# Decoded feed-forward weights stored whole in pass one, their block sums formed in pass two

## The chip, the core and the metric

The kernel runs on one core of one Trainium2 chip. The metric is the device time of one execution in microseconds, the median over several runs.

## What is computed

A transformer block with adaptive layer norm over 4 x 512 tokens of 1024 features: modulation vectors from a small matrix product, layer norm, a block-masked 1024 x 1024 product with a gated residual, layer norm, and a gated feed-forward network whose weights are stored as 4-bit codes with a scale for each 64 entries.

```python
mod = (_silu(L0_c) @ L0_wmod).reshape(L0_c.shape[0], 6, 1, -1)
sa, ca, ga, sb, cb, gb = (mod[:, 0], mod[:, 1], mod[:, 2], mod[:, 3], mod[:, 4], mod[:, 5])
...
h = _layernorm(x, axis=-1) * (1 + ca) + sa
x = x + ga * _L0_attn_ref(h, L0_attn_weight, L0_attn_mask)
h = _layernorm(x, axis=-1) * (1 + cb) + sb
x = x + gb * _L0_ffn_ref(h, L0_ffn_w1_q, ..., L0_ffn_w3_scale)
...
# in _L0_ffn_ref: w1, w2 of 2752 x 1024 and w3 of 1024 x 2752, decoded from codes and scales
h = jax.nn.silu(jnp.einsum('bsd,hd->bsh', x, w1)) * jnp.einsum('bsd,hd->bsh', x, w2)
return jnp.einsum('bsh,dh->bsd', h, w3)
```

## The kernel before

The five engines run programs written out by hand, each in its own order; they meet at semaphores (`wait_ge`, `then_inc`). Every DMA is issued by SyncE, whose queue is as strict in its order as the engines' programs: an issue that waits holds up all issues behind it. Each float32 product is made of three matmuls on a high part (rounded, made mostly by ScalarE) and a low part (the rest, made by VectorE).

The hidden dimension of 2752 is cut into 21 chunks of 128 (`FULL`) and a tail of 64.

**Pass one** (`up_group`) multiplies w1 and w2 with batches 0 and 1. For chunk c ScalarE decodes the codes of chunk c+1 by eight `lines` and VectorE scales and splits them (`finish`). The decoded tiles `RAW` (128 x 8 x 128 for w1 and for w2) are needed again in pass two, so what pass two wants of them is written to `t_d` in HBM.

**Pass two** (L1787) does the other two batches with seven block products for each chunk (`UP`: m5, m2, m1, m4, m6, m3, m7, a Strassen scheme over the two halves of the feature dimension, w1 against w2 and the two batches) in place of eight. Five of the seven weight operands are sums or differences of two blocks of 128 x 512, two (m4, m3) are a plain block. Before the change VectorE forms the sums in pass one (`sums`, buffers `TS`), and pass two loads one finished operand for each product (`load_stream`). They lie in buffers `TT[c % 2][i]`, i from 0 to 6 in the order of `UP`, each with a high part at its start and a low part behind it, over which the raw operand lands. ScalarE makes the high part (`stream_high`), VectorE the low part (`stream_low`, called a split below), one chunk ahead of TensorE. Of the seven results, ScalarE copies m5 and m2 out of PSUM (`copy_up`), VectorE adds the others to four tiles (`use_m1` two operations, `use_m4` two, `use_m6` one, `use_m3` two, `use_m7` one); then ScalarE applies silu (`silu_up`) and VectorE multiplies (`make_h_up`), in the next chunk. The input side of the seven products, `XC`, is formed once where pass two begins (`x_add`, `x_high`, `x_low`).

Beside this, pass two decodes w3: after the high parts of its chunk ScalarE runs eight steps on 128 x 1024 (`w3_lines`, L804), one block of w3 for each chunk and two in chunks 5 and 13 (`w3_jobs`); VectorE scales it (`w3_combine`, L1458); SyncE stores it, loads the next scales, and has the loads of streams 5 and 6 behind that store (`finish_w3` at i == 4).

ScalarE's program in a chunk of pass two is:

```python
silu_up(c - 1, 1)
silu_up(c - 1, 0)
stream_high(c + 1, 0)
copy_up(c, "m5")
for i in range(1, 4):
    stream_high(c + 1, i)
copy_up(c, "m2")
for i in range(4, NU):
    stream_high(c + 1, i)
...
for j in w3_jobs(c):
    w3_lines(j)
```

**The down projection** (`down_tile`) comes last. Its first loads, `t_raw` from w3 and `s_raw` from h, are issued in the last chunk of pass two behind the last `finish_w3`.

Of the kernel before, what the change touches and what calls it, by code (L numbers as in the profile page):

```python
# [23 lines left out]
P = 128  # L24
# [4 lines left out]
C = D // P  # L29
# [47 lines left out]
def adaln_kernel(nc, cT, x, w12q, w12s, w3q, w3s, wT, maskT, wmod, out):  # L77
# [41 lines left out]
    TS = [at(f"combined_{i}", [HALF_C, P], F32, 120 + 2 * i) for i in range(4)]  # L119
# [74 lines left out]
    t_d = nc.dram_tensor("t_d", (CH * NU * P, HALF_C * P), F32, kind="Internal").ap()  # L194
# [8 lines left out]
    ts_added, tt_hi, tt_lo = sem("ts_added"), sem("tt_hi"), sem("tt_lo")  # L203
    first_stored = sem("first_stored")
    ts_stored = [sem(f"ts_stored_{i}") for i in range(4)]
# [102 lines left out]
    FROM_W1, FROM_BOTH = ["m5"], ["m2", "m1", "m6", "m7"]  # L308
    FIRST_AT = 10
    SUMS = []  # L310
    for step in range(FULL):
        tile = step + 1
        SUMS += [(tile, "m2")] if tile == FULL else [(tile, name) for name in FROM_W1]
        if step == FIRST_AT:
            SUMS += [(0, name) for name in FROM_W1 + FROM_BOTH]
        if tile < FULL:
            SUMS += [(tile, name) for name in FROM_BOTH]

    def sums_through(n):
        return max(q for q, (tile, _) in enumerate(SUMS) if tile == n) + 1  # L320

# [79 lines left out]
    with block:  # L401

        @block.sync
        def _(sp):
# [10 lines left out]
            def load_codes(n, w):  # L415
                r = ring(n, w)
                if n >= 3:
                    sp.wait_ge(w12_lo, 2 * (n - 2) + 2)
                    sp.wait_ge(ts_added, sums_through(n - 2))
# [99 lines left out]
            def t_rows(n, name):  # L519
                row = (n * NU + UP_AT[name]) * P  # L520
                return t_d[row:row + P, :]

            def store_part(n, w, half):
                name = {0: "m3", 1: "m4"}[half]
# [6 lines left out]
                sp.dma_start(t_rows(n, name), src[:, half * HALF_C:(half + 1) * HALF_C, :].rearrange("p c k -> p (c k)")).then_inc(done, 16)  # L531
# [79 lines left out]
            for w in range(2):  # L611
                store_part(0, w, w)
            for c in range(FULL):
# [6 lines left out]
                store_part(n, 0, 0)  # L620
                if n == FULL:
                    store_part(n, 0, 1)
                store_sum(n, "m2" if n == FULL else "m5")
                if 1 <= c <= HALF_TILES - 2:
                    load_normed(c + 1)
                if c == FIRST_AT:
                    for name in FROM_W1 + FROM_BOTH:
                        store_sum(0, name)
                if n < FULL:
                    store_part(n, 1, 1)  # L630
                    if n + 1 < FULL:
                        load_s12(n + 1, 1)
                    store_sum(n, "m2")
                store_h(c, 0)
                if n < FULL:
                    store_sum(n, "m1")
                    store_sum(n, "m6")
                store_h(c, 1)
                if n < FULL:
                    store_sum(n, "m7")  # L640

                if c == FULL - 1:
                    sp.wait_ge(first_stored, 32)
                    for i in range(2):
                        load_stream(0, i)
                    for r in range(4):
                        sp.wait_ge(pure_stored[r], 16 * (12 if r == 2 else 10))
                        sp.wait_ge(ts_stored[r], 16 * len(range(r, len(SUMS), 4)))
                    for i in range(2, NU):
# [132 lines left out]
        def _(act):  # L782
# [163 lines left out]
            def stream_high(c, i):  # L946
                act.wait_ge(tt_loaded[c % 2][i], 16 * (c // 2 + 1))
                act.activation(TT[c % 2][i][0], TT[c % 2][i][2], ACT.Copy).then_inc(tt_hi, 1)  # L948

            def copy_up(c, name):  # L950
                p, i = c % 2, UP_AT[name]
                act.wait_ge(up_m_done, NU * c + i + 1)
                if c == 0:
                    for q in (2, 3):
                        act.wait_ge(ts_stored[q], 16 * len(range(q, len(SUMS), 4)))
                elif name == "m5" and c >= 2:
# [104 lines left out]
        def _(dve):  # L1061
# [15 lines left out]

            def sums(n, names):
                for name in names:
                    q = SUMS.index((n, name))  # L1080
                    if q >= 4:
                        dve.wait_ge(ts_stored[q % 4], 16 * (q // 4))
                    parts, sign = (((0, 0), (0, 1)), 1) if n == FULL else UP[UP_AT[name]][1:3]
                    if n == 0:
                        dve.wait_ge(raw_restored, 2)
                    src = [(RAW0[w] if n == 0 else RAW[ring(n, w)])[:, HALF_C * half:HALF_C * (half + 1), :] for w, half in parts]
                    dve.tensor_tensor(TS[q % 4][:], src[0], src[1], ALU.add if sign > 0 else ALU.subtract).then_inc(ts_added, 1)

# [258 lines left out]
            def early_x(c):  # L1347
# [4 lines left out]
                elif c == 14:  # L1352
                    dve.wait_ge(ts_added, sums_through(0))
# [4 lines left out]
            for c in range(FULL):  # L1358
                n = c + 1
                finish(n, 0)  # L1360
                sums(n, ["m2"] if n == FULL else FROM_W1)
                if 1 <= c <= HALF_TILES:
                    modulate_half(HALF_TILES + c - 1)
                if c == FIRST_AT:
                    sums(0, FROM_W1 + FROM_BOTH)
# [496 lines left out]
```

## Time and profile before

| | |
|---|---|
| median of 3 runs | 1634.79 us (1633.08 to 1635.11) |
| the profiled execution's own time | 1632.93 us |
| its span, mean granted clock of TensorE | 1630.9 us, 0.984 |
| TensorE matmul | 1553.4 us busy, 95% |
| VectorE | 1036.3 us busy, 64% |
| ScalarE | 988.0 us busy, 61% |
| DMA | 345.97 MB, mean 212 GB/s |

The span is the time from the first to the last instruction of the profiled execution. A busy share is a mean over stages: TensorE's is full in the three long stages and broken at the start and at the hand-overs from stage to stage. Matmuls of 128 x 512 overlap, so their pace is read from start to start and not from the length of one.

### The profile page before, as it was taken

The numbers are of one execution on the slowest core, as the hardware profiler recorded it, in microseconds if no ns is written. First come the engines' busy times: TensorE is split into PE (matmuls) and PEld (weight loads), VectorE is DVE, ScalarE is ACT, GpSimd is POOL, SyncE is SP. The second block draws the span as 40 slices with busy tenths as digits, with TensorE's granted clock in tenths as the row PEclk, the third lists the DMA queues.
The fourth block names the chain that finished last, engine by engine and source line by source line (L and its number), as shares of the span: only waits on it lengthen the run. The fifth ranks groups of instructions, "written<-read, shape, count | busy, mean of one in ns | idle before, by whom it ended". The sixth has DMA issues, their size and how long they took to land.

```text
span 1630.9 us, 19164 instructions
## 1 busy us (share of the span) xinstructions
PE 1553.4 (95%) x7216; PEld 1274.2 (78%) x7216; DVE 1036.3 (64%) x1494; ACT 988.0 (61%) x1280; POOL 10.6 (1%) x11
## 2 busy tenths in 40 slices
PE   2889999999999999999899999999969999999998
PEld 1667778888888888888688888888858888888886
DVE  3677687665545565444756566566676757867777
ACT  2445666898888888882777877877633333323320
POOL 1100000000000000000000000000000000000000
PEclk9899999999999999999999999999989999999999
DMA  9873421465446554442666766676587958958865
GB/s 370 336 257 136 169 90 63 174 213 178 166 156 207 174 174 153 151 152 97 212 202 194 232 210 215 207 234 230 174 309 301 315 176 298 360 180 298 308 220 196
DMA packets 170091, 345.97 MB, mean 212 GB/s; under 512 B 14728, under 2 KB 65288, under 8 KB 170000
## 3 DMA queue, kind: packets, MB, share of 16 engines
q1 hardware_dynamic: 170000, 344.76, 61.5%
q8 instruction: 57, 0.93, 0.2%
q14 instruction: 34, 0.28, 0.1%
HBM read 249.77 MB, written 94.93 MB: 211 GB/s over the span
## 4 chain that ended last, share of the span: by engine, by line
PE 63%; ACT 19%; DVE 10%; issue 4%; DMA 3%; SPq 1%; DVEq 0%; ACTq 0%
ACT w_raw L804 10%; PE ps L1746 9%; PE ps L1747 9%; PE ps L1748 9%; PE ps L1816 9%; PE ps L1817 9%; PE ps L1818 9%; ACT stream_hi L948 4%; DVE stream_lo L1380 2%; DVE up_c L1396 2%; DMA wmod<-wmod 2%; PE ps L1681 2%; PE ps L1683 2%; PE ps L1682 2%; PE ps L1645 2%
## 5 line engine op out<-in xcount | busy, mean ns | idle before, releaser
L794 ACT ACTIVATE w_raw<-w_raw 128x1024 f32<-128x1024 f32 x287 | 304.8, 1062 | 9.1
L1746 PE MATMUL ps<-ffn_in_hi,w_hi 128*128 128x512 f32 x688 | 268.6, 390 | 0.0
L1748 PE MATMUL ps<-ffn_in_hi,w_lo 128*128 128x512 f32 x688 | 267.8, 389 | 0.0
L1747 PE MATMUL ps<-ffn_in_lo,w_hi 128*128 128x512 f32 x688 | 267.7, 389 | 0.0
L1816 PE MATMUL ps<-t_hi,s_hi 128*128 128x512 f32 x616 | 240.5, 390 | 13.9 <-DVE s_lo L1504 13.9
L1760 PE MATMUL ps<-x_m_hi,stream_hi 128*128 128x512 f32 x604 | 236.5, 392 | 8.2 <-DVE x_m_lo L1345 4.8
L1817 PE MATMUL ps<-t_lo,s_hi 128*128 128x512 f32 x616 | 240.4, 390 | 0.0
L1818 PE MATMUL ps<-t_hi,s_lo 128*128 128x512 f32 x616 | 240.3, 390 | 0.0
L1762 PE MATMUL ps<-x_m_hi,stream_lo 128*128 128x512 f32 x604 | 236.3, 391 | 0.0
L1761 PE MATMUL ps<-x_m_lo,stream_hi 128*128 128x512 f32 x604 | 236.3, 391 | 0.0
L1010 ACT ACTIVATE s_hi<-s_raw 128x1408 fp32r<-128x1408 f32 x56 | 77.5, 1383 | 232.2 <-DVE s_raw L1499 189.5
L804 ACT ACTIVATE w_raw<-w_raw 128x1024 f32<-128x1024 f32 (+1 forms) x154 | 163.5, 1061 | 4.9
L1066 DVE SCALAR_TENSOR_TENSOR w_raw<-w_raw,w_scale 128x1024 f32<-128x1024 f32 x41 | 50.3, 1226 | 175.0 <-ACT w_raw L794 175.0
L1748 PEld LDWEIGHTS ps<-ffn_in_hi,w_lo 128*128 128x128 f32 x688 | 129.1, 188 | 27.0
L1746 PEld LDWEIGHTS ps<-ffn_in_hi,w_hi 128*128 128x128 f32 x688 | 129.2, 188 | 26.5
L1747 PEld LDWEIGHTS ps<-ffn_in_lo,w_hi 128*128 128x128 f32 x688 | 129.2, 188 | 26.5
L1816 PEld LDWEIGHTS ps<-t_hi,s_hi 128*128 128x128 f32 x616 | 116.1, 189 | 38.6 <-DVE s_lo L1504 14.3
L1760 PEld LDWEIGHTS ps<-x_m_hi,stream_hi 128*128 128x128 f32 x604 | 114.1, 189 | 33.6 <-issue 10.0
L1817 PEld LDWEIGHTS ps<-t_lo,s_hi 128*128 128x128 f32 x616 | 116.1, 188 | 24.1
L1818 PEld LDWEIGHTS ps<-t_hi,s_lo 128*128 128x128 f32 x616 | 116.0, 188 | 24.1
L1762 PEld LDWEIGHTS ps<-x_m_hi,stream_lo 128*128 128x128 f32 x604 | 114.1, 189 | 23.9
L1761 PEld LDWEIGHTS ps<-x_m_lo,stream_hi 128*128 128x128 f32 x604 | 114.0, 189 | 23.9
(127 smaller groups left out, 2097.3 us busy)
## 6 DMA issues: line engine op xcount, KB each, us to landing
s_raw<-h_d SPq DMA_DIRECT2D x96, 704.0 KB, 5.5
stream_raw<-t_d SPq DMA_DIRECT2D x150, 256.0 KB, 4.9
t_d<-combined SPq DMA_DIRECT2D x106, 256.0 KB, 2.6
wmod<-wmod SPq DMA_DIRECT2D x12, 2048.0 KB, 16.1
t_raw<-w_d SPq DMA_DIRECT2D x88, 256.0 KB, 6.4
w_codes<-w12q SPq DMA_DIRECT2D x41, 512.0 KB, 5.2
h_d<-h_tile SPq DMA_DIRECT2D x44, 256.0 KB, 2.4
w_d<-w_raw SPq DMA_DIRECT2D x22, 512.0 KB, 3.0
```

What stands on the lines that cost most here:

```text
L794: act.activation(RAWF[r], RAWF[r] if j else RQ[r][:], ACT.Prelu, bias=bias, scale=sign, alpha=slope).then_inc(line_ready, 1)
L804: act.activation(E3[p][0:rows, :], (E3 if j else E3Q)[p][0:rows, :], ACT.Prelu, bias=bias, scale=sign, alpha=slope).then_inc(w3_line, 1)
L1010: act.activation(SH[p][:], SR[p][:, 1], ACT.Copy).then_inc(s_hi, 1)
L1746: pe.matmul(acc, RH[r][:, k, :], HH[:, b, k, :], start=(k == 0), stop=False)
L1747: pe.matmul(acc, RH[r][:, k, :], HL[:, b, k, :], start=False, stop=False)
L1748: last = pe.matmul(acc, RL[r][:, k, :], HH[:, b, k, :], start=False, stop=(k == C - 1))
L1760: pe.matmul(acc, th[:, k, :], xh[:, k, :], start=(first and k == 0), stop=False)
L1761: pe.matmul(acc, th[:, k, :], xl[:, k, :], start=False, stop=False)
L1762: last = pe.matmul(acc, tl[:, k, :], xh[:, k, :], start=False, stop=(stop and k == HALF_C - 1))
L1816: pe.matmul(acc, SH[p][:, k, :], TH[i % 2][k][:], start=(k == 0), stop=False)
L1817: pe.matmul(acc, SH[p][:, k, :], TL[i % 2][k][:], start=False, stop=False)
L1818: last = pe.matmul(acc, SL[p][:, k, :], TH[i % 2][k][:], start=False, stop=(k == HC - 1))
```

## The change

Pass one stores the decoded tiles as they are, two of 512 KB for each chunk (`store_raw`), and forms no sums; `TS` and its semaphores are gone. In pass two each of the five combined operands is loaded as two raw blocks, one in the place of the low part as before, the other (`second`) in the place of the high part, and VectorE adds or subtracts them in place (`stream_add`) before ScalarE makes the high part over the second block. Each call of `stream_low` first does the add of the next operand in the order of the stream and then its own split. `stream_high` waits for the add (`tt_added`) where it waited for the load. Besides, `w3_combine` moves from behind `use_m6` to behind `use_m7`, and the first two loads of pass two no longer go ahead of the waits for pass one's stores. The programs of TensorE and ScalarE keep their order.

```diff
     def halves(name, kb, n):
...
-                at(name + "_raw", [HALF_C, n], F32, lo_kb)[:])
+                at(name + "_raw", [HALF_C, n], F32, lo_kb)[:], at(name + "_second", [HALF_C, n], F32, kb)[:] if n == P else None)
...
+    STREAM = [(c, i) for c in range(FULL) for i in range(NU)] + [(FULL, i) for i in (1, 3, 5)]
+
+    def weight_parts(c, i):
+        if c == FULL:
+            return {1: ((0, 0), (0, 1)), 3: ((0, 1),), 5: ((0, 0),)}[i]
+        return UP[i][1]
...
-            def store_part(n, w, half):
+            def store_raw(n, w):
...
-            def store_sum(n, name):
-                q = SUMS.index((n, name))
-                sp.wait_ge(ts_added, q + 1)
-                sp.dma_start(t_rows(n, name), TS[q % 4][:].rearrange("p c k -> p (c k)")).then_inc(ts_stored[q % 4], 16)
+                sp.dma_start(t_rows(n, w), src[:].rearrange("p c k -> p (c k)")).then_inc(done, 16)
...
             def load_stream(c, i):
                 if c >= 2:
                     sp.wait_ge(up_m_done, NU * (c - 2) + i + 1)
-                sp.dma_start(TT[c % 2][i][2].rearrange("p c k -> p (c k)"), t_rows(c, UP[i][0])).then_inc(tt_loaded[c % 2][i], 16)
+                for n, (w, half) in enumerate(weight_parts(c, i)):
+                    dst = TT[c % 2][i][2 + n]
+                    sp.dma_start(dst.rearrange("p c k -> p (c k)"), t_rows(c, w)[:, half * HALF:(half + 1) * HALF]).then_inc(tt_loaded[c % 2][i], 16)
...
             def stream_high(c, i):
-                act.wait_ge(tt_loaded[c % 2][i], 16 * (c // 2 + 1))
+                if len(weight_parts(c, i)) == 2:
+                    act.wait_ge(tt_added, stream_sums(c, i))
+                else:
+                    act.wait_ge(tt_loaded[c % 2][i], 16 * (c // 2 + 1))
                 act.activation(TT[c % 2][i][0], TT[c % 2][i][2], ACT.Copy).then_inc(tt_hi, 1)
...
             for c in range(FULL):
                 n = c + 1
                 finish(n, 0)
-                sums(n, ["m2"] if n == FULL else FROM_W1)
...
                 if n < FULL:
                     finish(n, 1)
-                    sums(n, FROM_BOTH[:1])
                 make_h(c, 0)
-                if n < FULL:
-                    sums(n, FROM_BOTH[1:3])
                 make_h(c, 1)
-                if n < FULL:
-                    sums(n, FROM_BOTH[3:])
-
-            def stream_low(c, i):
+
+            def stream_add(c, i):
+                parts = weight_parts(c, i)
+                if len(parts) == 2:
+                    dve.wait_ge(tt_loaded[c % 2][i], 32 * (c // 2 + 1))
+                    op = ALU.add if c == FULL or UP[i][2] > 0 else ALU.subtract
+                    t = TT[c % 2][i]
+                    dve.tensor_tensor(t[2], t[2], t[3], op).then_inc(tt_added, 1)
+
+            def stream_split(c, i):
                 dve.wait_ge(tt_hi, stream_at(c, i) + 1)
                 t = TT[c % 2][i]
                 dve.tensor_tensor(t[1], t[2], t[0].bitcast(F32), ALU.subtract).then_inc(tt_lo, 1)
 
+            def stream_low(c, i):
+                at_ = stream_at(c, i)
+                if at_ + 1 < len(STREAM):
+                    stream_add(*STREAM[at_ + 1])
+                stream_split(c, i)
+
+            stream_add(0, 0)
             for i in range(4):
                 stream_low(0, i)
...
                 use_m4(c)
                 use_m6(c)
-                for j in w3_jobs(c)[:1] if c else ():
-                    w3_combine(j)
                 for i in range(4, 6) if c else range(6):
                     stream_low(c + 1, i)
                 use_m3(c)
                 stream_low(c + 1, 6)
                 use_m7(c)
-                if c == 0:
-                    w3_combine(0)
-                for j in w3_jobs(c)[1:]:
+                for j in w3_jobs(c):
                     w3_combine(j)
```

What this makes of the order on the engines is seen at three places. In the names, `stream_04` is operand 4 of an even chunk, `stream_14` of an odd one, `raw`, `second`, `hi` and `lo` are its parts; line numbers are those of each kernel.

VectorE in a chunk of pass two, from `use_m6` on (`up_c...<-up_c...,ps`), before the change:

```order
L1396 TENSOR_TENSOR up_c22_1_169<-up_c22_1_169,ps 128x512
L1458 SCALAR_TENSOR_TENSOR w3_raw_0_174<-w3_raw_0_174,w3_scale_178 128x1024
L1380 TENSOR_TENSOR stream_04_lo_117<-stream_04_raw_118,stream_04_hi_116 128x512
L1380 TENSOR_TENSOR stream_05_lo_120<-stream_05_raw_121,stream_05_hi_119 128x512
L1396 TENSOR_TENSOR up_c22_1_169<-up_c22_1_169,ps 128x512
L1396 TENSOR_TENSOR up_c12_1_171<-up_c12_1_171,ps 128x512
L1380 TENSOR_TENSOR stream_06_lo_123<-stream_06_raw_124,stream_06_hi_122 128x512
L1396 TENSOR_TENSOR up_c11_1_167<-up_c11_1_167,ps 128x512
L1449 TENSOR_TENSOR up_c22_1_169<-up_c12_1_171,up_c22_1_169 128x512
L1449 TENSOR_TENSOR up_c21_1_173<-up_c11_1_167,up_c21_1_173 128x512
L1380 TENSOR_TENSOR stream_10_lo_126<-stream_10_raw_127,stream_10_hi_125 128x512
L1380 TENSOR_TENSOR stream_11_lo_129<-stream_11_raw_130,stream_11_hi_128 128x512
```

and with the change, where L1336 is the add and L1341 the split:

```order
L1364 TENSOR_TENSOR up_c22_1_179<-up_c22_1_179,ps 128x512
L1341 TENSOR_TENSOR stream_04_lo_117<-stream_04_raw_118,stream_04_hi_116 128x512
L1336 TENSOR_TENSOR stream_06_raw_126<-stream_06_raw_126,stream_06_second_127 128x512
L1341 TENSOR_TENSOR stream_05_lo_121<-stream_05_raw_122,stream_05_hi_120 128x512
L1364 TENSOR_TENSOR up_c22_1_179<-up_c22_1_179,ps 128x512
L1364 TENSOR_TENSOR up_c12_1_181<-up_c12_1_181,ps 128x512
L1336 TENSOR_TENSOR stream_10_raw_130<-stream_10_raw_130,stream_10_second_131 128x512
L1341 TENSOR_TENSOR stream_06_lo_125<-stream_06_raw_126,stream_06_hi_124 128x512
L1364 TENSOR_TENSOR up_c11_1_177<-up_c11_1_177,ps 128x512
L1426 SCALAR_TENSOR_TENSOR w3_raw_1_185<-w3_raw_1_185,w3_scale_188 128x1024
L1417 TENSOR_TENSOR up_c22_1_179<-up_c12_1_181,up_c22_1_179 128x512
L1417 TENSOR_TENSOR up_c21_1_183<-up_c11_1_177,up_c21_1_183 128x512
```

Add 6 now stands between the splits of operands 4 and 5, behind `use_m6`; the add of operand 0 for the chunk after stands ahead of split 6; and the combine has moved behind `use_m7`, directly ahead of the two multiplications of `make_h_up`.

VectorE where pass two begins, from the first split to the first `x_add`, before the change:

```order
L1380 TENSOR_TENSOR stream_00_lo_105<-stream_00_raw_106,stream_00_hi_104 128x512
L1380 TENSOR_TENSOR stream_01_lo_108<-stream_01_raw_109,stream_01_hi_107 128x512
L1380 TENSOR_TENSOR stream_02_lo_111<-stream_02_raw_112,stream_02_hi_110 128x512
L1380 TENSOR_TENSOR stream_03_lo_114<-stream_03_raw_115,stream_03_hi_113 128x512
L1335 TENSOR_TENSOR x_m1_raw_154<-ffn_in_raw_00_51,ffn_in_raw_11_54 128x2048
```

and with the change:

```order
L1336 TENSOR_TENSOR stream_00_raw_102<-stream_00_raw_102,stream_00_second_103 128x512
L1336 TENSOR_TENSOR stream_01_raw_106<-stream_01_raw_106,stream_01_second_107 128x512
L1341 TENSOR_TENSOR stream_00_lo_101<-stream_00_raw_102,stream_00_hi_100 128x512
L1336 TENSOR_TENSOR stream_02_raw_110<-stream_02_raw_110,stream_02_second_111 128x512
L1341 TENSOR_TENSOR stream_01_lo_105<-stream_01_raw_106,stream_01_hi_104 128x512
L1341 TENSOR_TENSOR stream_02_lo_109<-stream_02_raw_110,stream_02_hi_108 128x512
L1336 TENSOR_TENSOR stream_04_raw_118<-stream_04_raw_118,stream_04_second_119 128x512
L1341 TENSOR_TENSOR stream_03_lo_113<-stream_03_raw_114,stream_03_hi_112 128x512
L1297 TENSOR_TENSOR x_m1_raw_164<-ffn_in_raw_00_51,ffn_in_raw_11_54 128x2048
```

Four adds have come between, and the last of them is that of operand 4, which needs the eighth and ninth load.

SyncE around the store of a decoded w3 block in pass two, before the change:

```order
L554 DMA stream_04_raw_118<-t_d 128x512
L562 DMA w3_codes_1_177<-w3q 128x1024
L572 DMA w3_d<-w3_raw_0_174 128x1024
L567 DMA w3_scale_178<-w3s 64x1024 x2
L554 DMA stream_05_raw_121<-t_d 128x512
L554 DMA stream_06_raw_124<-t_d 128x512
L554 DMA stream_10_raw_127<-t_d 128x512
```

and with the change:

```order
L543 DMA stream_04_raw_118<-t_d 128x512
L543 DMA stream_04_second_119<-t_d 128x512
L551 DMA w3_codes_0_186<-w3q 128x1024
L561 DMA w3_d<-w3_raw_1_185 128x1024
L556 DMA w3_scale_188<-w3s 64x1024 x2
L543 DMA stream_05_raw_122<-t_d 128x512
L543 DMA stream_06_raw_126<-t_d 128x512
L543 DMA stream_06_second_127<-t_d 128x512
L543 DMA stream_10_raw_130<-t_d 128x512
L543 DMA stream_10_second_131<-t_d 128x512
```

The two loads behind the w3 store are three now, and operand 0 of the next chunk takes two as well.

## Rows read from the trace of the kernel before

**Rows 1.** Busy time by stretch: from:to, length, busy per engine, clock, DMA, GB/s

```profile
475.00:660.00 185.00, 185.00 (x822) 153.31 (x821) 98.66 (x121) 152.65 (x157) 0.00 (x0) 1.00 0.51 169
802.44:1157.33 354.89, 354.89 (x1567) 293.85 (x1566) 217.73 (x334) 278.98 (x370) 0.00 (x0) 1.00 0.67 215
1066.00:1085.00 19.00, 19.00 (x85) 15.75 (x84) 11.96 (x19) 14.52 (x20) 0.00 (x0) 1.00 0.85 284
```

**Rows 2.** What TensorE waited for: total us, times, longest

```profile
PE ps L1816 <- DVE s_lo L1504: 13.9, 1, 13.9
PE ps L1760 <- DVE x_m_lo L1345: 4.8, 3, 1.9
```

**Rows 3.** ScalarE in order of time, one chunk: start, length, [idle before <-releaser]

```profile
842.77 0.64 ACT L972 ACTIVATE up_c<-up_c 128x512 f32<-128x512 f32 x1 [3.69 <-DVE up_c L1396]
...
847.07 0.59 ACT L962 ACTIVATE up_c<-ps 128x512 f32<-128x512 f32 x1
847.54 1.67 ACT L948 ACTIVATE stream_hi<-stream_raw 128x512 fp32r<-128x512 f32 x3
849.11 1.06 ACT L804 ACTIVATE w_raw<-w_codes 128x1024 f32<-128x1024 int32 x1
...
867.85 1.06 ACT L804 ACTIVATE w_raw<-w_codes 128x1024 f32<-128x1024 int32 x1
```

**Rows 4.** VectorE in order of time, the same chunk

```profile
847.74 1.29 DVE L1396 TENSOR_TENSOR up_c<-ps,up_c 128x512 f32<-128x512 f32 x2 [0.89 <-ACT up_c L962]
848.95 1.28 DVE L1380 TENSOR_TENSOR stream_lo<-stream_raw,stream_hi 128x512 fp32r<-128x512 f32 x2
850.15 1.88 DVE L1396 TENSOR_TENSOR up_c<-up_c,ps 128x512 f32<-128x512 f32 x3
857.85 1.23 DVE L1458 SCALAR_TENSOR_TENSOR w_raw<-w_raw,w_scale 128x1024 f32<-128x1024 f32 x1 [5.83 <-ACT w_raw L804]
858.99 1.29 DVE L1380 TENSOR_TENSOR stream_lo<-stream_raw,stream_hi 128x512 fp32r<-128x512 f32 x2
```

**Rows 5.** TensorE in order of time: start of chunk 1, end of the tail

```profile
796.63 0.63 PE L1762 MATMUL ps<-x_m_hi,stream_lo 128*128 128x512 f32 x1
797.06 0.46 PE L1760 MATMUL ps<-x_m_hi,stream_hi 128*128 128x512 f32 x1
...
1188.61 0.39 PE L1762 MATMUL ps<-x_m_hi,stream_lo 128*128 128x512 f32 x1
```

**Rows 6.** Groups by line, shapes apart: the in-place add of the down projection

```profile
L1511 DVE TENSOR_TENSOR t_raw<-t_raw 128x512 f32<-128x512 f32 x55 | 37.4, 688 | 25.4 <-DMA t_raw<-w_d 25.4
```

**Rows 7.** SyncE's queue in order of time, after a combine

```profile
860.76 1.55 SPq L554 DMA_DIRECT2D stream_raw<-t_d  x3
```

**Rows 8.** DMA issues of the page: count, size, median us to landing

```profile
stream_raw<-t_d SPq DMA_DIRECT2D x150, 256.0 KB, 4.9
```

**Rows 9.** ScalarE in order of time, start of pass two

```profile
759.01 0.63 ACT L948 ACTIVATE stream_hi<-stream_raw 128x512 fp32r<-128x512 f32 x1 [14.39 <-DMA stream_raw<-t_d]
759.94 0.63 ACT L948 ACTIVATE stream_hi<-stream_raw 128x512 fp32r<-128x512 f32 x1 [0.29 <-DMA stream_raw<-t_d]
...
793.84 1.04 ACT L804 ACTIVATE w_raw<-w_codes 128x1024 f32<-128x1024 int32 x1
```

**Rows 10.** VectorE in order of time, start of pass two

```profile
763.22 4.49 DVE L1335 TENSOR_TENSOR x_m_raw<-ffn_in_raw,ffn_in_raw 128x2048 f32<-128x2048 f32 x2
...
790.32 2.29 DVE L1345 TENSOR_TENSOR x_m_lo<-ffn_in_raw,x_m_hi 128x2048 fp32r<-128x2048 f32 x1 [1.38 <-ACT x_m_hi L944]
792.53 1.88 DVE L1396 TENSOR_TENSOR up_c<-up_c,ps 128x512 f32<-128x512 f32 x3
```

**Rows 11.** ScalarE: decode of the last w3 rows

```profile
1157.33 1.06 ACT L804 ACTIVATE w_raw<-w_codes 64x1024 f32<-64x1024 int32 x1
```

**Rows 12.** TensorE: first matmul of the down projection

```profile
1202.87 0.80 PE L1816 MATMUL ps<-t_hi,s_hi 128*128 128x512 f32 x1 [13.87 <-DVE s_lo L1504]
```

**Rows 13.** First line of the page

```profile
span 1630.9 us, 19164 instructions
```

More of the change, by code:

```diff
@@ L202, in adaln_kernel @@
     raw_restored = sem("raw_restored")
-    ts_added, tt_hi, tt_lo = sem("ts_added"), sem("tt_hi"), sem("tt_lo")
+    tt_added, tt_hi, tt_lo = sem("tt_added"), sem("tt_hi"), sem("tt_lo")
     first_stored = sem("first_stored")
-    ts_stored = [sem(f"ts_stored_{i}") for i in range(4)]
     pure_stored = [sem(f"pure_stored_{i}") for i in range(4)]
@@ L306, in group_bank, with stream_sums @@
         return g % 6
[L308 to L320, printed above, removed]
+    STREAM = [(c, i) for c in range(FULL) for i in range(NU)] + [(FULL, i) for i in (1, 3, 5)]
[3 more added lines that the diff above has]
+        return UP[i][1]
+    def stream_sums(c, i):
+        return sum(len(weight_parts(*s)) == 2 for s in STREAM[:stream_at(c, i) + 1])
     H0 = 2 * CH
@@ L517, in _, with t_rows @@
                         load_codes(1, w)
-            def t_rows(n, name):
-                row = (n * NU + UP_AT[name]) * P
+            def t_rows(n, w):
+                row = (n * 2 + w) * P
                 return t_d[row:row + P, :]
-            def store_part(n, w, half):
-                name = {0: "m3", 1: "m4"}[half]
+            def store_raw(n, w):
                 if n == 0:
@@ L619, in _ @@
                     load_s12(n + 1, 0)
[L620 to L623, printed above, removed]
+                store_raw(n, 0)
                 if 1 <= c <= HALF_TILES - 2:
                     load_normed(c + 1)
-                if c == FIRST_AT:
-                    for name in FROM_W1 + FROM_BOTH:
-                        store_sum(0, name)
                 if n < FULL:
-                    store_part(n, 1, 1)
+                    store_raw(n, 1)
                     if n + 1 < FULL:
                         load_s12(n + 1, 1)
-                    store_sum(n, "m2")
                 store_h(c, 0)
-                if n < FULL:
-                    store_sum(n, "m1")
-                    store_sum(n, "m6")
                 store_h(c, 1)
-                if n < FULL:
-                    store_sum(n, "m7")
                 if c == FULL - 1:
                     sp.wait_ge(first_stored, 32)
-                    for i in range(2):
-                        load_stream(0, i)
                     for r in range(4):
-                        sp.wait_ge(pure_stored[r], 16 * (12 if r == 2 else 10))
-                        sp.wait_ge(ts_stored[r], 16 * len(range(r, len(SUMS), 4)))
-                    for i in range(2, NU):
+                        sp.wait_ge(pure_stored[r], 16 * (11 if r == 2 else 10))
+                    for i in range(NU):
                         load_stream(0, i)
@@ L952, in copy_up @@
                 act.wait_ge(up_m_done, NU * c + i + 1)
-                if c == 0:
-                    for q in (2, 3):
-                        act.wait_ge(ts_stored[q], 16 * len(range(q, len(SUMS), 4)))
-                elif name == "m5" and c >= 2:
+                if name == "m5" and c >= 2:
                     act.wait_ge(h_made, H0 + 2 * (c - 1))
@@ L1076, in restore_first @@
                 dve.tensor_tensor(RAW0[w][:], RH[w][:].bitcast(F32), RL[w][:].bitcast(F32), ALU.add).then_inc(raw_restored, 1)
[L1078 to L1087, printed above, removed]
             def early_combine(n):
```

13 lines of the change are left out of this document (2 added, 11 removed).

## The prediction

> **What bounds the kernel now.** I read the stretches first, then TensorE's waits, then one chunk of pass two engine by engine, then the two hand-overs. In pass one TensorE is busy in every microsecond of the stretch and also in the middle of pass two, at the full clock [rows 1]. Its idle time near the change is small: 4.8 us behind `x_low` where pass two begins, 13.9 us behind `s_low` where the down projection begins [rows 2]. So no time can be won in pass one, and little in pass two; the question is what the change puts on the path.
>
> In pass two the matmuls follow each other every 0.2267 us (391.55 us between the two full-speed rows for 1727 steps), so a chunk of 84 takes TensorE 19.04 us, and from chunk 1 (797.06) the tail chunk is due at 1177.9 [rows 5]. ScalarE and VectorE turn in a loop of their own beside it. ScalarE starts the w3 decode of a chunk at 849.11 and the next one at 867.85, a period of 18.74 us [rows 3]; VectorE combines at 857.85, 8.74 us after the decode began [rows 4], and ScalarE's silu of a chunk had waited 3.69 us for VectorE [rows 3]. The loop is a little quicker than TensorE, so nothing there reaches the matmuls. Call W(c) the start of the decode in chunk c: W(0) is 793.84 [rows 9] and W(19) is 1157.33 [rows 11], 363.5 us apart. What follows pass two hangs on W(19): the store of the last w3 rows waits for its combine, SyncE issues the `t_raw` and `s_raw` loads behind that store, and the first matmul of the down projection stands at 1202.87 [rows 12], 45.5 us after W(19), the execution's end [rows 13] 473.6 us after it.
>
> **Pass one and the moved adds.** 106 adds of 128x512 leave VectorE's pass one and 106 appear in pass two. The nearest row, an in-place add of that form, takes 0.69 us [rows 6], and VectorE starts such work every 0.60 us when nothing holds it (1.20 us for two) [rows 4]. In pass one they lay beside a TensorE that never waits [rows 1], so their removal is worth nothing, and so are the stores that become two of 512 KB per chunk in place of seven of 256 KB. A gain there is excluded because there is no idle time to take.
>
> **The new loop in pass two.** The change makes ScalarE's high part of block 6 wait for an add that stands on VectorE behind `use_m6` of the chunk, and ScalarE starts the w3 decode only after that high part. VectorE comes to `use_m6` only after it has combined the decode before. Decode and VectorE's chain, which ran side by side, now follow each other. From W(c-1), with 0.60 per VectorE operation, 0.52 per high part on ScalarE (1.57 for three [rows 3]) and 0.05 to 0.08 from one engine to the other (the copy at 847.07 ends at 847.66 and `use_m1` begins at 847.74 [rows 3, 4]):
> combine starts 8.74, next 9.88 (1.14 [rows 4]); two `make_h_up` to 11.08; add 1 and split 0 to 12.28; add 2 is done at 12.97, its high part starts at 13.02; high parts 2 and 3 to 14.06; copy of m2 and hand-over to 14.73; two of `use_m1`, split 2, add 4, split 3, two of `use_m4`, `use_m6`, split 4 are nine operations, to 20.13; add 6 done and handed over 20.87; high part 6, 0.52 more.
> W(c) = W(c-1) + 21.35, rounded between my hand-over times, against TensorE's 19.04. Chunks 5 and 13 decode two w3 blocks and add 8.7 each, with nothing beside it. So W'(19) - W'(0) = 19 x 21.35 + 2 x 8.7 = 423.1, which is 59.6 us more than 363.5. Bounds: without any hand-over time the cycle is 21.2 (+57), with 0.1 at every crossing and 0.62 per operation 21.8 (+68).
>
> TensorE has one chunk of cover: split 0 of the next chunk is done at W(c-1) + 12.4. The cover is used up at about chunk 4 (W'(2) + 12.4 = 860.5, when chunk 4 would be due at 859); from then on TensorE idles some 2.3 us ahead of each chunk, and longer ahead of the chunks after 5 and 13.
>
> **The hand-over into pass two.** Before, `x_add` began at 763.22, right after four splits [rows 10]; the first two loads had been turned at 759.01 and 759.94, one per 0.93 us [rows 9]. Now VectorE has add 4 in front of `x_add`, and that is the ninth load: 759.0 + 8 x 0.93 = 766.4, then an add and a split, so `x_add` at 767.6, 4.4 us later (1.5 if the nine loads cost 0.5 each, 8 at 1.4). Add 6 lies in the chain after it, 0.6. The first add of chunk 1 falls into the 1.38 us that `x_low` of m7 waits for ScalarE and costs nothing [rows 10]; without that wait it would be 0.6. So `use_m4` at 792.53 [rows 10] moves to 797.5, its three operations end at 799.3, eight more stand before add 6 (804.1), and with hand-over and high part W'(0) = 805.4, 11.6 us later than before (range 9 to 15).
>
> **w3 combine behind `use_m7`.** By itself it frees VectorE, which stood 5.8 us in front of the combine [rows 4], and costs a later unlocking of SyncE. Behind it on SyncE stand the w3 store, the scales and the loads of blocks 5 and 6. Before, the first of these loads was issued at 860.76, 2.9 us after the combine began [rows 7]; now W + 11.65, the last of three about W + 12.7, and with the median of 4.9 us to landing [rows 8] W + 17.6. Add 6 wants it at W + 20.1. So it is hidden, by 2.5 us.
>
> **The loads.** A chunk moves 12 blocks of 256 KB instead of 7, 1.3 MB more. At 215 GB/s a period of 18.74 us carries 4.0 MB; 5.3 MB in 21.35 us is 250 GB/s, and a stretch with 284 GB/s showed 0.85 of the engines' time [rows 1]. Not the bound.
>
> **The end.** The tail can start when its first split is done, about W'(19) + 12.8, and ends 10.9 us later. The down projection is unlocked from W(19) as before; VectorE gets there up to 3.6 us earlier because combine no longer stands before three splits' worth of work, but the loads behind it were issued back to back, so I take 1 us (0 to 3.6). TensorE then idles about 21 us there instead of 13.9.
>
> **Sum.** 11.6 + 59.6 - 1 = +70 us. The profiled execution took 1632.93 us, 1.9 below the median of the runs, which is 0.1%; the forecast for the median is 1634.8 + 70 = 1705 us.
>
> **Rivals.**
> *Cover holds (6%).* The adds run in VectorE's idle time and only the start of pass two is paid: +5 to +12, 1642 us. For it: VectorE is busy 217.7 of 354.9 us [rows 1], so 0.6 x 5 adds fit by quantity. Against it: the order above, not the quantity. The Trainium skill, page Perfetto Trace Analysis, section Identifying the Most-Contended Engine, says that a kernel gains by work on its most contended engine. By that rule, with TensorE full and VectorE at 61%, the adds would be free and the time this rival's.
> *Loads late (7%).* The landing of block 6 takes 2.5 us more than the median, and each microsecond beyond that is paid in some 19 chunks: at 8 us of landing +0.6 a chunk, 1716; at 10 us +2.6, 1754.
> *The clock (4%).* After a wait TensorE ran at 1.2 GHz for a spell, a matmul each 0.43 us (796.63 to 797.06 [rows 5]); eight such cost 1.6 us. With a gap of 2.3 us in each chunk this disappears in the gap, since the loop and not TensorE sets the pace. If the spell were 24 matmuls, 4.8 us, TensorE would need 23.8 us a chunk: 2.5 more for 16 chunks, 1745. [...]
> *Faster (3%).* The combine blocked VectorE for 5.8 us a chunk. If add 6 were always there before its high part is due, ScalarE would follow TensorE: W(19) could be the start of chunk 19 (1139.9) plus two products 5.4 and four operations 2.1, 1147.4, ten microseconds earlier, less 5 at the start: 1630 us. It decides only if add 6 gets past `use_m6`, the chunk's fifth product, which the program order forbids.
>
> **Numbers.** Loop as worked out 80%, with 1697 to 1718 as its own range from the bounds above. Cover holds and faster lie below, the others above; with the near half of the late loads the range is 1688 to 1722. Measurement tells about 0.2% (3 us) from no change. Slower by more than that: 0.95 (loop, late loads, clock, most of cover holds); within it 0.02 (the rest of cover holds); faster 0.03.
>
> **What would show it.** Right: in pass two the decode's first row comes every 21.3 us; ScalarE waits for adds, some 2.6 us ahead of high part 4 and 2.6 us ahead of high part 6; VectorE waits about 5.8 us in front of the combine and then goes straight to `make_h_up`; TensorE waits about 2.3 us a chunk for a split; pass one unchanged to a microsecond; about 21 us before the down projection. Wrong: the decode starting right behind the copy of m2, or VectorE waiting for loads in each chunk, or TensorE full in pass two.

## The result and the profile after

The changed kernel takes 1703.85 us (median of 4 runs, 1703.41 to 1706.23) where the kernel before takes 1634.95 (4 runs): ratio 1.0425, 95% interval 1.0407 to 1.0443, slower by 69 us. The forecast was 1705, range 1688 to 1722. The profiled execution took 1704.21 us, 71.3 more than the one of before.

The busy time by stretch of the changed kernel, to be read beside [rows 1]:

```profile
475.00:660.00 185.00, 185.00 (x822) 153.32 (x821) 70.82 (x75) 152.75 (x157) 0.00 (x0) 1.00 0.38 127
802.44:1157.33 354.89, 317.89 (x1348) 257.87 (x1347) 231.17 (x364) 247.67 (x319) 0.00 (x0) 0.96 0.72 237
```

In pass one VectorE has lost 28 us of work in 185 and the time is the same: TensorE was full and is full. In pass two TensorE does 1348 matmuls in the same 354.89 us where it did 1567, and no engine is at its limit: VectorE, which got the additions, is busy 65%. Who waits for whom shows more. One chunk of ScalarE in order of time:

```profile
881.45 0.63 ACT L924 ACTIVATE stream_hi<-stream_raw 128x512 fp32r<-128x512 f32 x1 [1.06 <-DVE stream_raw L1336]
882.66 1.15 ACT L924 ACTIVATE stream_hi<-stream_raw 128x512 fp32r<-128x512 f32 x2 [0.57 <-DVE stream_raw L1336]
883.71 0.58 ACT L935 ACTIVATE up_c<-ps 128x512 f32<-128x512 f32 x1
886.90 1.15 ACT L924 ACTIVATE stream_hi<-stream_raw 128x512 fp32r<-128x512 f32 x2 [2.61 <-DVE stream_raw L1336]
890.50 0.64 ACT L924 ACTIVATE stream_hi<-stream_raw 128x512 fp32r<-128x512 f32 x1 [2.45 <-DVE stream_raw L1336]
891.04 1.05 ACT L777 ACTIVATE w_raw<-w_codes 128x1024 f32<-128x1024 int32 x1
```

and VectorE in the same chunk:

```profile
878.38 1.23 DVE L1426 SCALAR_TENSOR_TENSOR w_raw<-w_raw,w_scale 128x1024 f32<-128x1024 f32 x1 [5.71 <-ACT w_raw L777]
879.53 1.29 DVE L1417 TENSOR_TENSOR up_c<-up_c,up_c 128x512 f32<-128x512 f32 x2
880.73 0.69 DVE L1336 TENSOR_TENSOR stream_raw<-stream_raw,stream_second 128x512 f32<-128x512 f32 x1
...
884.38 1.29 DVE L1364 TENSOR_TENSOR up_c<-ps,up_c 128x512 f32<-128x512 f32 x2 [1.15 <-issue]
...
889.78 0.69 DVE L1336 TENSOR_TENSOR stream_raw<-stream_raw,stream_second 128x512 f32<-128x512 f32 x1
...
899.78 1.22 DVE L1426 SCALAR_TENSOR_TENSOR w_raw<-w_raw,w_scale 128x1024 f32<-128x1024 f32 x1 [5.71 <-ACT w_raw L777]
```

The loop can be followed with a finger: addition 6 at 889.78, high part 6 at 890.50, the decode at 891.04, VectorE stands 5.71 us and combines at 899.78, and 11.4 us later it reaches addition 6 again. Most of these 11.4 us are VectorE's own operations. In their middle it stands 1.15 us ahead of `use_m1` (884.38). The profile puts this down to issue, but `use_m1` waits for the copy of m2, which ScalarE begins at 883.71, behind high parts 2 and 3, and which takes 0.58 us. So these three operations of ScalarE are part of the loop. In the kernel before, the silu waited for VectorE [rows 3]; now all waits of ScalarE in the chunk, 6.7 us, name an addition. What TensorE waited for, beside [rows 2]:

```profile
PE ps L1724 <- DVE stream_lo L1341: 44.2, 17, 10.6
PE ps L1780 <- DVE s_lo L1468: 21.3, 1, 21.3
...
PE ps L1724 <- DVE x_m_lo L1307: 6.7, 3, 3.3
```

The first line is new. The second has grown from 13.9, although the same work stands ahead of it: what it waits for hangs on the last decode as before, and only TensorE's cover is gone.

### The profile page after: what moved, and what is told of

Its sections match the earlier page's. It is cut to its first block, busy times and chain, and to the rows that moved or that the text cites. A ratio compares the mean times of both kernels' runs of the same rounds, so it can differ in the third digit from the quotient of the medians.

```text
span 1702.6 us, 19153 instructions
## 1 busy us (share of the span) xinstructions
PE 1571.1 (92%) x7216; PEld 1281.9 (75%) x7216; DVE 1034.2 (61%) x1494; ACT 992.7 (58%) x1280; POOL 10.6 (1%) x11
## 4 chain that ended last, share of the span: by engine, by line
PE 60%; DVE 17%; ACT 15%; issue 4%; DMA 3%; SPq 1%; DVEq 0%; ACTq 0%
ACT w_raw L777 11%; PE ps L1710 9%; PE ps L1712 9%; PE ps L1711 9%; PE ps L1780 8%; PE ps L1781 8%; PE ps L1782 8%; DVE up_c L1364 4%; DVE stream_raw L1336 3%; DMA wmod<-wmod 2%; PE ps L1645 2%; PE ps L1647 2%; PE ps L1646 2%; DVE stream_lo L1341 2%; PE ps L1609 2%
## 5 line engine op out<-in xcount | busy, mean ns | idle before, releaser
L1724 PE MATMUL ps<-x_m_hi,stream_hi 128*128 128x512 f32 x604 | 244.3, 404 | 54.5 <-DVE stream_lo L1341 44.2
L1725 PE MATMUL ps<-x_m_lo,stream_hi 128*128 128x512 f32 x604 | 241.5, 400 | 0.0
L1726 PE MATMUL ps<-x_m_hi,stream_lo 128*128 128x512 f32 x604 | 240.8, 399 | 0.0
L924 ACT ACTIVATE stream_hi<-stream_raw 128x512 fp32r<-128x512 f32 x150 | 89.9, 626 | 160.7 <-DVE stream_raw L1336 156.2
```

Source lines behind the costliest of these rows:

```text
L1724: pe.matmul(acc, th[:, k, :], xh[:, k, :], start=(first and k == 0), stop=False)
L1725: pe.matmul(acc, th[:, k, :], xl[:, k, :], start=False, stop=False)
L1726: last = pe.matmul(acc, tl[:, k, :], xh[:, k, :], start=False, stop=(stop and k == HALF_C - 1))
```

## The experiments

The theory: a loop of program order (decode, combine, gate products, additions 1 and 2, ScalarE's high parts 2 and 3 and copy of m2, VectorE's operations up to addition 6, high part 6, next decode) takes 21.4 us where TensorE needs 19.04. Against it stand the amount of VectorE work, the twelve loads in place of seven, and the later combine by itself.

**The same extra work in two places.** One more VectorE instruction of 0.60 us, written to a spare buffer, in each of 19 chunks (2 to 20 in the edit; both expectations count 18): ahead of split 0 (inside the loop), or ahead of split 6 (behind addition 6, where VectorE goes on to wait for the decode). In `stream_split` (with `i == 6` in the other kernel):

```
+                if i == 0 and 2 <= c < FULL:
+                    dve.tensor_tensor(SPARE[:], t[2], t[0].bitcast(F32), ALU.subtract)
                 dve.tensor_tensor(t[1], t[2], t[0].bitcast(F32), ALU.subtract).then_inc(tt_lo, 1)
```

> The changed kernel with one more VectorE instruction of an addition's size (0.60 us, written to spare memory and used by nobody) in each of 18 chunks, ahead of the split of block 0, between the gate products and addition 2. By the loop of order it is paid in full: period 22.0, time 1703.9 + 18 x 0.60 = 1714.7 (1712 to 1717). Rival, the loop isn't through VectorE's additions at that place: 1704.

> The same 18 instructions of the same size, ahead of the split of block 6 instead: behind addition 6, with the 5.7 us wait for the decode still to come. VectorE does exactly as much as in the kernel with the extra ahead of split 0. By the loop of order they cost nothing: period 21.4, time 1704 (1702 to 1706). Rival, the amount of VectorE work sets the time: 1714, as the other.

Measured: 1715.95 us inside the loop (ratio 1.0508, 1.0494 to 1.0523) and 1703.81 in the wait (1.0436, 1.0422 to 1.0450), 12 us apart for the same 19 instructions. VectorE's combine and the extra, in the kernel with the extra inside the loop:

```profile
881.28 1.23 DVE L1429 SCALAR_TENSOR_TENSOR w_raw<-w_raw,w_scale 128x1024 f32<-128x1024 f32 x1 [5.70 <-ACT w_raw L778]
...
884.23 0.68 DVE L1343 TENSOR_TENSOR spare<-stream_raw,stream_hi 128x512 f32<-128x512 f32 x1
```

and the extra and the next combine, with the extra behind addition 6:

```profile
892.09 0.68 DVE L1343 TENSOR_TENSOR spare<-stream_raw,stream_hi 128x512 f32<-128x512 f32 x1
...
899.07 1.23 DVE L1429 SCALAR_TENSOR_TENSOR w_raw<-w_raw,w_scale 128x1024 f32<-128x1024 f32 x1 [5.10 <-ACT w_raw L778]
```

The wait for the decode gave exactly what the extra took, 5.71 to 5.10. Inside the loop the wait stayed 5.70 and the decodes moved from 21.39 to 21.98 us apart. From W(0) to W(19), the prediction's names for the starts of the first and last decode, that kernel took 434.78 us (806.59 to 1241.37) where the changed kernel took 423.65: 11.1 us, or 19 times 0.59. With the extra in the wait it took 423.75. So the time is set by the length of one chain and not by VectorE's load.

**Without the additions, all loads kept.** `stream_add` is taken out and the high parts wait for both loads. The kernel leaves out the block sums; one raw block stands in the place of each:

```
-                if len(weight_parts(c, i)) == 2:
-                    act.wait_ge(tt_added, stream_sums(c, i))
-                else:
-                    act.wait_ge(tt_loaded[c % 2][i], 16 * (c // 2 + 1))
+                act.wait_ge(tt_loaded[c % 2][i], 16 * len(weight_parts(c, i)) * (c // 2 + 1))
```

> Of the changed kernel, the VectorE additions that form the block sums in pass two are taken out; the high parts wait for both of their loads directly. All loads stay (two blocks where there were two), the w3 combine stays behind the last step of the chunk. Left out: the sums themselves, so products m1, m2, m6, m7 use one raw block each. If the loop through the additions set the pace (decode, combine, two gate products, addition 1, split 0, addition 2, high part 2, ...), nothing of it is left: TensorE bound again, period 19.04 us per chunk, W'(19)-W'(0) near 362, time 1633 (1626 to 1638). Rival, the second loads are what costs (72% DMA, landing 5.9 us): the period stays above 21, time 1690 or more. Rival, the later combine alone costs: period between 19.5 and 21, time 1650 to 1690.

Measured 1645.42 (1.0073, 1.0058 to 1.0088): 57 of the 69 us are gone, but 12 remain where I expected none. ScalarE in that kernel:

```profile
892.04 0.63 ACT L921 ACTIVATE stream_hi<-stream_raw 128x512 fp32r<-128x512 f32 x1 [3.03 <-DMA stream_raw<-t_d]
894.29 0.63 ACT L921 ACTIVATE stream_hi<-stream_raw 128x512 fp32r<-128x512 f32 x1 [1.61 <-DMA stream_second<-t_d]
894.82 1.04 ACT L777 ACTIVATE w_raw<-w_codes 128x1024 f32<-128x1024 int32 x1
```

A second loop lay under the first: combine, w3 store, the loads of blocks 5 and 6 behind it on SyncE, high part 6, decode. It takes 19.1 to 19.6 us in most chunks, a little more than TensorE, and eats the cover until TensorE waits once, 5.38 us, in the chunk after the second double decode (1073.22). This second loop was tested by issuing those loads ahead of the store, in the same kernel:

```
-                    if jobs and i == 4:
-                        finish_w3(jobs[0])
-                    if len(jobs) == 2 and i == 6:
-                        finish_w3(jobs[1])
+                    if jobs and i == 4 and jobs[0] + 1 < CH:
+                        load_w3_codes(jobs[0] + 1)
+                    if jobs and i == 6:
+                        store_w3(jobs[0])
+                        if jobs[0] + 1 < CH:
+                            load_s3(jobs[0] + 1)
+                        for j in jobs[1:]:
+                            finish_w3(j)
```

> The changed kernel without the block sums' additions (left out: the sums; one raw block is used in their place) as in the first run, which came out 12 us above the kernel before where none was expected, and SyncE issues the stream loads 5 and 6 ahead of the w3 store. If those 12 us are a loop from the combine through the w3 store and the two late loads to high part 6 and the next decode, 8 to 9 of them go: 1636 (1632 to 1640); what is left is the later start of pass two. Rival, the higher DMA traffic or the landing times themselves: 1645.

Measured 1627.31 (0.9958, 0.9944 to 0.9971), below the expected range. The second loop was worth all of the 12 us and 6 more: I had kept a term of 3 us for the start of pass two, and left out that a faster ScalarE also shortens TensorE's wait ahead of the down projection (6.9 us where it was 14.1). The twelve loads of a chunk cost nothing in the loop once those of blocks 5 and 6 stand ahead of the store.

**The order of loads in the changed kernel itself.** The same SyncE edit and no other:

> Of the changed kernel, only SyncE's order is changed: the stream loads 5 and 6 are issued ahead of the w3 store, which waits for the combine; VectorE's order stays. The kernel with additions 4 and 6 early gained 33 us and this reordering on top of it another 40. If the loop through addition 6 behind VectorE's steps is what binds here and the loop through the loads lies 1.3 us or more under it, as the prediction had it, nothing moves: period 21.4, time 1704 (1700 to 1707). Rival, the late loads bind as well: period near 20 and 1675 or less.

Measured 1703.59 (1.0426, 1.0411 to 1.0440), as expected. ScalarE's waits there are [2.61] and [2.45] as above. The loop through the additions hides the one through the loads.

**The order on VectorE.** Additions 4 and 6 of the next chunk go ahead of `use_m1`; the later `stream_low` calls become plain splits:

```
                     for i in range(2):
                         stream_low(c + 1, i)
+                    for i in (4, 6):
+                        stream_add(c + 1, i)
                 use_m1(c)
```

> Of the changed kernel, only VectorE's order is changed: additions 4 and 6 of the next chunk stand ahead of the use of m1, where VectorE has slack. High part 6 then doesn't wait for the 6 us of steps ahead of addition 6, but addition 6 waits for its own two loads, which SyncE issues behind the wait for the w3 combine. If the loop of order is the cause, the period falls from 21.4 to about 20.1 and the time to 1679 (1672 to 1686): the loop now closes through those loads. Rival, the amount of work or of traffic: 1704. Rival, additions 4 and 6 were the whole loop: 1635.

Measured 1670.45 (1.0222, 1.0205 to 1.0239), below the expected range by 1.6 us: single chunks took 19.9 us on the mean and not 20.1. VectorE now waits where it was said it would:

```profile
885.50 0.69 DVE L1336 TENSOR_TENSOR stream_raw<-stream_raw,stream_second 128x512 f32<-128x512 f32 x1 [4.12 <-DMA stream_second<-t_d]
```

> As the kernel with additions 4 and 6 ahead of the use of m1, and SyncE issues the stream loads 5 and 6 ahead of the w3 store, which waits for the combine. No work is added or taken out. If the loop of order is the cause, both ways round it are cut: the loop through the rest is 16.2 us, TensorE's 19.04 sets the pace, time 1630 (1626 to 1635), below the kernel before because VectorE's combine no longer holds ScalarE's decode. Rival, amount of VectorE work (231 us of 355 busy) or of traffic: 1690 or more. Rival, some other wait of about 1 us per chunk: 1650.

Measured 1630.58 (0.9980, 0.9971 to 0.9989). Both loops are cut, with all 106 additions and all loads in place. The decodes come every 16.10 us while there is slack and then follow TensorE. One order without the other is worth 0.3 us (loads) or 33 us (additions), and both together 73: limits that lie under each other don't add.

**The decode first.** ScalarE decodes ahead of high parts 4 to 6, from chunk 1 on:

```
                     copy_up(c, "m2")
-                    for i in range(4, NU):
-                        stream_high(c + 1, i)
                 for j in w3_jobs(c):
                     w3_lines(j)
+                if c >= 1:
+                    for i in range(4, NU):
+                        stream_high(c + 1, i)
```

> Of the changed kernel, only ScalarE's order within a chunk is changed (from chunk 1 on): the w3 decode stands ahead of the high parts 4 to 6 of the next chunk, so that it no longer stands behind the VectorE additions 4 and 6. Nothing is added or taken out. If a loop of order sets the pace: decode at copy m2 and hand-over, 14.7 us behind the decode before, then the three high parts and their waits; next chunk is bounded by the decode, by high 6 and by its successor, period about 19.9 (above TensorE's 19.04), a double chunk 28.5, time 1676 (1670 to 1683). Rival, the amount of VectorE or DMA work sets the pace: period stays 21.4, time 1704. Rival, the loop is fully broken: TensorE bound, 1635.

Measured 1699.25 (1.0398, 1.0382 to 1.0414): a miss. The single chunks took 19.87 us, as expected; the two with two decodes took 39.35 and 40.04 instead of 28.5. In the first of them ScalarE and VectorE read:

```profile
912.50 1.06 ACT L777 ACTIVATE w_raw<-w_codes 128x1024 f32<-128x1024 int32 x1 [3.85 <-DMA w_codes<-w3q]
```

```profile
926.53 1.22 DVE L1427 SCALAR_TENSOR_TENSOR w_raw<-w_raw,w_scale 128x1024 f32<-128x1024 f32 x1
933.50 1.23 DVE L1427 SCALAR_TENSOR_TENSOR w_raw<-w_raw,w_scale 128x1024 f32<-128x1024 f32 x1 [5.75 <-DMA w_scale<-w3s]
```

3.85 for the second block's codes, 5.75 for its scales, which are loaded only behind the first combine, and 1.14 for that combine are 10.7 of the 10.85 us. With the old order kept in those two chunks (`late = c >= 1 and len(w3_jobs(c)) == 1`):

> The changed kernel with the decode ahead of the high parts 4 to 6, except in the two chunks with two decodes, which keep the old order. Decode first everywhere gave 1699.3 where 1676 was expected: its single chunks took 19.87 us as expected, but the two double ones 39.35 instead of 28.5, because the second decode waited 3.85 us for its codes and the second combine 5.75 us for its scales. If that is the whole of the miss, the double chunks now take 30 and the time is 1699.3 - 2 x 9.4 = 1680.5 (1676 to 1684). Rival, something else in the order: 1690 or more.

Measured 1678.30 (1.0277, 1.0263 to 1.0291), 21 us less and within the expected range: the miss was those two chunks.

**The later combine alone, in the kernel before.**

```
-                for j in w3_jobs(c)[:1] if c else ():
-                    w3_combine(j)
...
-                if c == 0:
-                    w3_combine(0)
-                for j in w3_jobs(c)[1:]:
+                for j in w3_jobs(c):
                     w3_combine(j)
```

> The kernel before, with one part of the change alone: the w3 combine moved behind the use of m7 in every chunk. Block sums are still formed in pass one. Theory (the combine's place does harm only together with additions that the high parts wait for): TensorE bound as before, VectorE no longer waits for the decode in the middle of a chunk, the decode runs up to 19.04 us per chunk or faster, and the gap ahead of the down projection falls from 13.9 us towards 4: time 1626 (1622 to 1632). Rival, the later combine closes a loop of its own through the w3 store and the loads 5 and 6 (the kernel without additions lost 5 us that way): 1640 to 1650. Rival, the combine's place carries the loss by itself: 1660 or more.

Measured 1627.33 (0.9961, 0.9949 to 0.9974): this part of the change is a gain of 7 us when it stands alone. The last decode starts at 1148.52 where it started at 1157.33 [rows 11], and TensorE's wait ahead of the down projection is

```profile
PE ps L1812 <- DVE s_lo L1500: 7.3, 1, 7.3
```

instead of 13.9 [rows 2]; I had expected 4. The rival with the store is not seen with one load in place of two: the first decodes there are 17.5 to 18.1 us apart (829.50, 847.62, 865.58, 883.12), under TensorE's 19.04.

**The hand-over.** On top of the kernel of 1630.58, SyncE issues chunk 0's loads ahead of the last h store of pass one:

```
                 store_h(c, 0)
-                store_h(c, 1)
                 if c == FULL - 1:
                     ...
                     for i in range(NU):
                         load_stream(0, i)
+                store_h(c, 1)
```

> The kernel with additions 4 and 6 early and loads ahead of the w3 store (1630.6), and at the end of pass one SyncE issues the fourteen parts' loads of chunk 0 ahead of the last h store, which waits for VectorE at 756.9: they go out near 752 and not at 757.6. VectorE idled 4.95 us for the first of them, and is then busy nearly without a gap until the first use of m4. Theory: VectorE's whole stretch moves 4 to 5 us earlier, so do TensorE's four waits for x low parts: 1626 (1623 to 1629). Rival, the x additions wait for TensorE's group of 761.5 anyway, and the gap ahead of the down projection takes back what is won: 1630.

Measured 1625.72 (0.9947, 0.9933 to 0.9961), as expected. And the same edit on the kernel before with the late combine:

> The kernel before with the w3 combine moved late (1627.3) and chunk 0's loads ahead of the last h store of pass one, as in the kernel of 1625.7. It says whether that kernel's 8 us belong to the whole storage or only to the two orders. There TensorE waited for x low parts for 4.4 us; VectorE waited 4.0 us ahead of its first split. Theory, orders only: the first split starts 4 us earlier but the x additions wait for TensorE's group of 761.5, so 1 to 2 us are won: 1626 (1623 to 1628). Rival: 4 us or more, 1622.

Measured 1623.35 (0.9946, 0.9932 to 0.9960). It is within the expected range, but won more than the 1 to 2 us expected: 4.0 us by the medians, 2.5 by the two ratios, each against its own runs of the kernel before. The x additions start at 760.33, where their wait for TensorE's group ends, and not at 763.22 [rows 10]. I had put the end of that group at 761.5 from the kernel of 1630.58. In its trace the first matmul of pass two stands at 766.96, 1.4 us later than here (765.57), so the group was never that late in this kernel. The two best kernels are thus 0.5% faster than the one before, one with sums in pass one and one with sums in pass two, and their ratios can't be told apart. Storing the weights whole buys no time here and, with the orders set for it, costs none. Pass two of the one with the additions in it (1625.72):

```profile
802.44:1157.33 354.89, 354.89 (x1567) 293.85 (x1567) 281.49 (x441) 297.24 (x384) 0.00 (x0) 1.00 0.86 282
```

VectorE is 79% busy and DMA at 0.86, more than in the slow kernel, and TensorE without a gap.

## Why the prediction was right, point by point

*The loop.* Forecast W(c) = W(c-1) + 21.35 and 8.7 for a second decode; measured 21.39 and 8.57 (912.44, 942.41, 963.80). The terms of the forecast, added up as they are listed, give 21.39 too (20.87 and 0.52); 21.35 is a rounding that costs 0.8 us over the 19 chunks. W'(19) - W'(0) was 423.65 against 423.1. ScalarE waits 2.61 ahead of high part 4 and 2.45 ahead of high part 6, VectorE 5.71 ahead of the combine, as worked out. That the cause is this loop and not the amount of work is shown by the pair with the extra instruction, by the kernel with both orders changed, and by the one without additions. That additions 4 and 6 could not simply have kept the combine ahead of them is argued from the order of the instructions (each would wait for the other) and wasn't tried.

*The hand-over.* x_add was forecast at 767.6, came at 767.29; use_m4 797.5 and 797.20; addition 6 804.1 and 804.19; W'(0) 805.4 and 805.45. The rows:

```profile
760.53 0.69 DVE L1336 TENSOR_TENSOR stream_raw<-stream_raw,stream_second 128x512 f32<-128x512 f32 x1 [4.99 <-DMA stream_second<-t_d]
...
766.08 0.69 DVE L1336 TENSOR_TENSOR stream_raw<-stream_raw,stream_second 128x512 f32<-128x512 f32 x1
...
767.29 4.49 DVE L1297 TENSOR_TENSOR x_m_raw<-ffn_in_raw,ffn_in_raw 128x2048 f32<-128x2048 f32 x2
```

*The cover.* It was to be used up when chunk 4 begins, at 860.5; the wait with which TensorE's idling starts, 1.72 us, ends at 860.67. From then on the gaps are 2.05 us and not 2.3, and only 0.4 in every second or third chunk, for the reason in the last section. Behind the two chunks with two decodes they are 10.6 us.

*The end.* Forecast -1; measured nothing: W(19) to the first matmul of the down projection is 45.50 us (1229.10 to 1274.60) against 45.54. The gap was forecast at 21 and is 21.31.

*The sum.* 11.6 + 60.2 + 0 = 71.8 on the profiled execution, against 71.7 in its span and 71.3 in its own time. The medians are 69 apart; the kernel before ran at 1634.95 in the median and its profiled execution at 1632.93. The forecast of 1705 lies 1.2 us from the measured median. A profiled execution and its median lie up to 2 us apart here, so the last microsecond of that closeness is luck.

*Rivals.* "Cover holds" failed: TensorE was the full engine, VectorE had room, and the time rose 4%. The Trainium skill (page Perfetto Trace Analysis, section Identifying the Most-Contended Engine) says to optimize the engine with the highest occupancy first. Read as if work on any other engine were free, as this rival does, that disagrees with this trace. "Loads late" didn't happen, though landing rose from 4.9 us to 5.9 and 6.4 for the two kinds of load. The term that was off is the spare time of the loads, forecast at 2.5 us. Their issue came as forecast: the last load of block 6 went out at W + 12.76 (869.65 to 882.41), forecast W + 12.7.

```profile
882.41 0.43 SPq L543 DMA_DIRECT2D stream_second<-t_d  x1
```

What was too small is the time to landing, taken from the median of 4.9 us in the kernel before. This load took 6.3 us and landed at 888.7, and addition 6 began at 889.78, so 1.1 us were to spare. The same load of the other chunks took 5.4 to 6.3 us nearly everywhere, which leaves 1.1 to 2.0. With additions 4 and 6 moved, addition 6 waited for those loads and came 9.6 us behind the combine (875.94 to 885.50); in the changed kernel it comes 11.4 behind it. That difference of 1.8 us fits, and the loads' own loop, 19.9 us there on the mean, lay 1.5 under the one that bound. "The clock" did not cost; see below.

## What to carry to other kernels

Ask of an operation that moves to another place not how busy its engine is there, but who waits for it and what that engine must pass in program order before it gets there; if the answer comes back to the operation, add up the loop and compare it with the period of the engine that sets the pace. Two engines that issue in order and wait for each other twice in a period form such a loop, and each 0.6 us in it is paid in each period, while the same 0.6 us outside it is free. When one loop is cut, look at once for the next under it: here the second was 1.5 us shorter, and cutting either alone hid most of what both were worth.

## What the hardware showed that was not expected

I had expected a spell at 1.2 GHz behind each gap of 2 us. There was none behind most of them; in one chunk the rows of TensorE are

```profile
976.22 0.50 PE L1724 MATMUL ps<-x_m_hi,stream_hi 128*128 128x512 f32 x1 [2.05 <-DVE stream_lo L1341]
976.56 0.40 PE L1725 MATMUL ps<-x_m_lo,stream_hi 128*128 128x512 f32 x1
...
997.62 0.50 PE L1724 MATMUL ps<-x_m_hi,stream_hi 128*128 128x512 f32 x1 [2.07 <-DVE stream_lo L1341]
...
999.25 0.63 PE L1726 MATMUL ps<-x_m_hi,stream_lo 128*128 128x512 f32 x1
999.67 0.63 PE L1724 MATMUL ps<-x_m_hi,stream_hi 128*128 128x512 f32 x1
...
1019.01 0.50 PE L1724 MATMUL ps<-x_m_hi,stream_hi 128*128 128x512 f32 x1 [0.47 <-DVE stream_lo L1341]
```

Behind the wait of 2.05 us the matmuls go on at full speed, behind the next, 2.07 us, some eight run 0.43 us apart (1.2 GHz), and the gap after that chunk is 0.47 instead of 2.06: the slow spell costs 1.6 us of idle time and none of the kernel's. The granted clock of the two chunks is 1.00 (976.2 to 997.2) and 0.92 (997.6 to 1018.6). Such spells came behind some of like gaps and not behind others; what decides wasn't tried. The Trainium skill (page TensorE: Matmul & The Clock Gate, section HAM oscillation — how this bites in real kernels) describes a kernel that waited some 3 to 5 us for a DMA in each tile and came back at the low clock every time. The waits here are shorter, and the spell came in some chunks only. Their cost is not gone everywhere: the kernel without additions fell to a mean of 0.94 around its one wait of 5.38 us (1050 to 1110), with nothing to absorb it.
